# State space layer: where a batch's row adds and statistics stand, and which activation tables it uses

## The reference, cut to what matters

```python
x = x + _L0_ffn_ref(_layernorm(x), ...)        # top-2 experts: two rows per token come back
x = x + _L1_attn_a_ref(_layernorm(x), ...)     # the state space layer
x = x + _L1_ffn_ref(_layernorm(x), ...)

def _layernorm(x, axis=-1, eps=1e-05):
    return (x - mean) / sqrt(var + eps)

def _L1_attn_a_ref(x, W_in, conv_w, conv_b, W_x, W_dt, b_dt, A_log, D, W_out):
    xi, z = split(x @ W_in.T)
    u = silu(causal_conv4(xi) + conv_b)
    Bm, Cm = split(u @ W_x.T)
    delta = softplus(u @ W_dt.T + b_dt)
    dA = exp(delta * -exp(A_log));  dB = delta * Bm
    h_t = dA_t * h_{t-1} + u_t * dB_t;  y_t = sum(h_t * c_t)     # scan over the tokens
    return ((y + u * D) * silu(z)) @ W_out.T
```

## Time and profile before

| | us |
|---|---|
| median of three runs | 4240.26 |
| the three runs | 4235.73, 4240.26, 4248.27 |
| the profiled execution, its own time | 4241.42 |
| its span, first to last instruction | 4239.6 |
| busy in the span: TensorE, VectorE, ScalarE, GpSimd | 3643.4, 2895.8, 1905.3, 1622.4 |
| mean granted TensorE clock | 0.941 |

### The profile page before, as it was taken

How to read it: one execution, slowest core, us unless ns; L and a number is a source line. 1 busy time by engine, 2 the same in 40 slices (tenths; PEclk the granted TensorE clock), 3 DMA queues, 4 the chain that set the end, 5 groups by cost and what they waited for, 6 DMA issues and landing times. The chain is left out here.

```text
span 4239.6 us, 59957 instructions
## 1 busy us (share of the span) xinstructions
PE 3643.4 (86%) x19161; PEld 2603.3 (61%) x19224; DVE 2895.8 (68%) x5457; ACT 1905.3 (45%) x3879; POOL 1622.4 (38%) x1493
## 2 busy tenths in 40 slices
PE   5888877898499999998799578878789899999998
PEld 3555566787488888877688534444556455554666
DVE  5777556565576666646556457787789767676898
ACT  3555543443355555545334244443323266666332
POOL 3776625443566666524544211010101354441000
PEclk8999978999799999998899879899999899999999
DMA  5999802554100000001355400000300444451000
GB/s 134 298 285 264 256 32 86 160 157 155 63 17 17 19 19 22 14 5 49 104 169 168 147 20 18 13 20 1 60 0 11 97 101 112 98 116 34 11 15 15
DMA packets 228873, 358.33 MB, mean 85 GB/s; under 512 B 36482, under 2 KB 132850, under 8 KB 221810
## 3 DMA queue, kind: packets, MB, share of 16 engines
q1 hardware_dynamic: 204038, 265.38, 21.1%
q0 software_dynamic: 24544, 89.36, 8.4%
HBM read 173.82 MB, written 172.20 MB: 82 GB/s over the span
## 5 line engine op out<-in xcount | busy, mean ns | idle before, releaser
L2848 DVE TENSOR_REDUCE ab_nmx<-banks 128x1 f32<-128x512 f32 x512 | 329.2, 684 | 134.3 <-PE banks L2635 131.7
L2779 ACT ACTIVATE ab_pt<-banks 128x512 f32<-128x512 f32 x512 | 283.1, 600 | 159.5 <-PE banks L2645 151.3
L1714 POOL TENSOR_TENSOR lb_pq<-lb_pq,lb_rr 128x512 f32<-128x512 f32 x192 | 206.5, 1079 | 307.0 <-DVE lb_rr L1581 303.9
L1456 ACT ACTIVATE lb_pq<-banks,lb_nmx 128x256 f32<-128x256 f32 x384 | 178.9, 471 | 228.6 <-DVE lb_nmx L1576 225.7
L2645 PE MATMUL banks<-ab_qT,ab_kT 128*128 128x512 f32 x512 | 251.1, 494 | 5.7 <-ACT ab_pt L2779 5.7
L1576 DVE TENSOR_REDUCE lb_nmx<-banks 128x2 f32<-128x512 f32 x192 | 131.2, 683 | 157.0 <-PE banks L1308 155.7
L358 ACT ACTIVATE da_pt<-banks 128x512 f32<-128x512 f32 (+1 forms) x384 | 179.0, 536 | 122.2 <-PE banks L270 117.8
L2635 PE MATMUL banks<-ab_kT,ab_qT 128*128 128x512 f32 x512 | 207.6, 408 | 16.9 <-DVE ab_nmx L2848 12.2
L644 POOL DMA_INDIRECT mb_xi<-moe_ys,moe_b_place x64 | 65.0, 1015 | 388.6 <-DVE mb_uT L2095 340.7
L285 PE MATMUL banks<-da_pt,da_vx 128*64 128x512 f32 (+3 forms) x1024 | 165.7, 469 | 34.0 <-POOL da_pt L578 30.4
L2424 PE MATMUL banks<-w_f_dT,f_hT 128*128 128x256 f32 x768 | 181.2, 387 | 4.0 <-ACT f_hT L2460 4.0
(11 more groups left out here) (532 smaller groups left out, 11230.8 us busy)
## 6 DMA issues: line engine op xcount, KB each, us to landing
moe_xs<-zero SPq DMA_DIRECT2D x71, 512.0 KB, 11.0
moe_ys<-zero SPq DMA_DIRECT2D x71, 512.0 KB, 10.9
moe_a_w_raw<-in_moe_w SPq DMA_DIRECT2D x48, 512.0 KB, 3.9
moe_b_w_raw<-in_moe_w SPq DMA_DIRECT2D x48, 512.0 KB, 3.9
da_spill<-da_hi SPq DMA_DIRECT2D x128, 128.0 KB, 2.4
ab_spill<-ab_hi SPq DMA_DIRECT2D x128, 128.0 KB, 2.4
ab_qT<-ab_spill POOLq DMA_DIRECT2D x32, 392.0 KB, 5.7
ab_kT<-ab_spill POOLq DMA_DIRECT2D x32, 392.0 KB, 5.5
```

What stands on the lines that cost most here:

```text
L1456: nc.scalar.activation(pq[:, n % RING, t, :], ps[:, S_BANK + n % 2, 2 * P * t:2 * P * t + 2 * P], ACT.Exp, bias=nmx[:, n % RING, t:t + 1], ...
L1714: nc.gpsimd.tensor_tensor(pq[:, n % RING, :, :], pq[:, n % RING, :, :], bcast(rr[:, n % RING, :], 2, 2 * P), ALU.mult).then_inc(s_p, 1)
L2779: nc.scalar.activation(pt[:, s % RING, :], ps[:, EXP_BANK + s % 3, :], ACT.Exp, scale=AB_D ** -0.5).then_inc(s_e, 1)
L2848: nc.vector.tensor_reduce(nmx[:, g % 2, col:col + 1], ps[:, MAX_BANK + n % 3, :], op=ALU.max, axis=AX.X, negate=True).then_inc(s_mx, 1)
```

## The change

The job `add` is split: its half k of batch b now stands at -19 + k, that is phases 5 and 6, and the first half waits for the batch's eight gathers. The statistics of the new rows become a job `stats` of their own in phase 7, behind `scan`, where the whole add stood. The statistics of finished rows, which followed `out` 1 in phase 4, become a job `later` at slot 22, that is phase 10 of the next batch, behind `direct` of tile 3; the last batch's come after the loop. `fetch` moves from -18 to -21. `root` computes `exp(-0.5 * ln(var + eps))` into `rstd`, and `scale` has no reciprocal any more. The table set with exponential and logarithm is loaded by name at the start and after each batch's last `u`.

```diff
-    vector_table = [(-17, "add", 0), (-15, "scale", 0), (-12, "conv", 0), ...
-                    ... (-3, "parts", 0), (1, "parts", 1)]
-    pool_table = [(-18, "fetch", 0)]
+    vector_table = [(-19, "add", 0), (-18, "add", 1), (-17, "stats", 0), (-15, "scale", 0), (-12, "conv", 0), ...
+                    ... (-3, "parts", 0), (1, "parts", 1),
+                    (22, "later", 0)]
+    pool_table = [(-21, "fetch", 0)]
...
                 def u(b, m):
...
+                    if m == MB_EC - 1:
+                        nc.scalar.preload_act_table_set("natural_log_exp_and_others")
...
                 def root(b, i):
                     act.wait_ge(s_stats, b + 1)
-                    nc.scalar.activation(core.std[:, b, :], core.mv[:, b, :, 1], ACT.Sqrt, bias=core.eps[:, :],
-                                         scale=1.0).then_inc(s_root, 1)
+                    nc.scalar.activation(core.std[:, b, :], core.mv[:, b, :, 1], ACT.Ln, bias=core.eps[:, :], scale=1.0)
+                    act.drain()
+                    nc.scalar.activation(core.rstd[:, b, :], core.std[:, b, :], ACT.Exp, scale=-0.5).then_inc(s_root, 1)
...
                 act.wait_ge(core.loaded["mb"], core.loads["mb"])
+                nc.scalar.preload_act_table_set("natural_log_exp_and_others")
...
-                def add(b, i):
-                    dve.wait_ge(s_fetch, 16 * TOPK * NT * (b + 1))
-                    for k in range(TOPK):
-                        dve.drain()
-                        choice.add(b, k, fetched).then_inc(s_added, 1)
-                    dve.drain()
+                def add(b, k):
+                    if k == 0:
+                        dve.wait_ge(s_fetch, 16 * TOPK * NT * (b + 1))
+                    choice.add(b, k, fetched).then_inc(s_added, 1)
+                    dve.drain()
+
+                def row_stats(b, i):
                     token_stats(core, dve, b)
                     dve.drain().then_inc(s_stats, 1)
 
+                def later_stats(b, i):
+                    token_stats(core, dve, b)
+
                 def scale(b, i):
                     dve.wait_ge(s_root, b + 1)
-                    nc.vector.reciprocal(core.rstd[:, b, :], core.std[:, b, :])
-                    dve.drain()
...
                 def empty(job):
...
-                        if i == 1:
-                            dve.drain()
-                            token_stats(core, dve, b)
-                            dve.drain()
...
                         if kind != "conv":
                             jobs_of[kind](b, i)
+                dve.drain()
+                later_stats(B - 1, 0)
```

More of the change, by code:

```diff
@@ L1805, in state_space @@
     table += [(3 * i + 4, "turn", i) for i in range(NT)] + [(10, "out", 0), (15, "out", 1)]
-    vector_table = [(-17, "add", 0), (-15, "scale", 0), (-12, "conv", 0), (-11, "conv", 1), (-11, "conv", 2), (-10, "conv", 3),
-                    (-6, "delta", 0), (-5, "scan", 0), (-4, "state", 0), (-4, "cdp", 0), (-3, "parts", 0), (1, "parts", 1)]
-    pool_table = [(-18, "fetch", 0)]
+    vector_table = [(-19, "add", 0), (-18, "add", 1), (-17, "stats", 0), (-15, "scale", 0), (-12, "conv", 0), (-11, "conv", 1), (-11, "conv", 2), (-10, "conv", 3),
+                    (-6, "delta", 0), (-5, "scan", 0), (-4, "state", 0), (-4, "cdp", 0), (-3, "parts", 0), (1, "parts", 1),
+                    (22, "later", 0)]
+    pool_table = [(-21, "fetch", 0)]
     scalar_table = [(-16, "root", 0), (-15, "normal", 0), (-11, "u", 0), (-11, "u", 1), (-10, "u", 2), (-9, "u", 3), (-6, "decay", 0), (-3, "parts", 0), (1, "parts", 1)]
@@ L2190, in finish @@
                     nc.vector.tensor_tensor(gz[b % 2][:, i, :], gz[b % 2][:, i, :], v1[:, :], ALU.mult).then_inc(s_y, 1)
-                jobs_of = {"add": add, "scale": scale, "conv": conv, "delta": step, "scan": scan, "cdp": first_sum, "state": state,
+                jobs_of = {"add": add, "stats": row_stats, "later": later_stats, "scale": scale, "conv": conv, "delta": step, "scan": scan, "cdp": first_sum, "state": state,
                            "parts": parts}
```

## The result

The changed kernel took 4250.59 us (median of 16 runs, 4241.73 to 4257.21), the kernel before 4241.66 (16 runs, 4235.73 to 4249.94): a ratio of 1.0020, 95% interval 1.0013 to 1.0027, or +5.5 to +11.5 us. I had said 4243.6 within 4230 to 4256, and no change that a measurement tells from none (0.3%) as likeliest. It came out so: the increase is clear of the noise but stays under 0.3%. It is some two and a half times my sum of +3.4 us, though. The profiled execution took 4253.90 us (span 4252.1, clock 0.938).

A forecast was written before the change was run, and what follows sets the result against it. A loop of waits, no full engine, was taken to set the period. Gather wait +9.0, moved statistics +1.0, front -5.4 and tail -1.2 make +3.4 us: 4244.8 profiled, 4243.6 as median, range 4230 to 4256.

The forecast's parts named there:

- The gather term: Phase 5: VectorE waits some 6.0 us for gathered rows; 28.2 against 26.74 us to the product, +9.0 in six periods.
- 0.96 throughout: Sign in the profile after: every gather issue on GpSimd takes 0.96 us, none the 1.29 of the last issue before.
- `finish` alone: GpSimd's gather issues: the long ones go away with VectorE's `finish` out of their way; otherwise six periods cost 4.2 us more.
- The moved statistics: Phase 10, before `out`: 2.3 us return, mostly hidden; 0.2 us in each of five periods, +1.0.
- the cover: Phase 10: TensorE's `x` transposes also wait for ScalarE's copies, hiding later-emptied `out`; without it 0.6 us each.
- The front: Stage start to second shift: fewer table loads ahead of the second gather, no reciprocal; -5.4 us (-4.5 to -6.5).
- one table set: ScalarE: five loads of 1.28 us a batch become two; worth nothing more in the six periods, but counting at the front.
- The tail: Last two batches: VectorE paces the last one, so statistics taken from phase 4 are partly gained; -1.2 us.
- (a): Faster rival, phase 5: gathered rows are there when VectorE comes, six periods give -15; 4219.7 us, chance 0.05.
- (b): Slower rival: longer idle TensorE keeps `out` and what follows at low clock, 2 us in six periods; 4255.6, chance 0.12.
- (c): Rival: the table set isn't shared, logarithm and exponential still load, the front loses its gain; 4247, chance 0.03.
- the bounds: Low and high ends of the terms for periods, statistics and front; together said to put the sum at 0 to +10 us.

The follow-up runs named there:

- adds_late: The changed kernel with the two add groups one slot later each (-18 and -17); 4233.76 us, 0.9981 of before.
- own_rows: The changed kernel with fetched rows in buffers free earlier, so gathers no longer wait for the last `conv`; 4224.90 us, 0.9957 of before.
- second pair: Second profiles of the two unchanged programs, the kernel before and the changed kernel; 4248.03 and 4253.90 us.
- first pair: First profiles of the kernel before and the changed kernel; profiled executions 4241.42 and 4253.90 us.
- best: The changed kernel with fetched rows in buffers free earlier and the statistics of finished rows in slot 23 instead of 22; 4221.79 us, 0.9951 of before.
- split_alone: The kernel before with only the adds split and the new rows' statistics in slots of their own, gathers listed at -21; 4253.41 us, 1.0020 of before.
- later_alone: The kernel before with only the statistics of finished rows moved from phase 4 to phase 10 of the next batch; 4251.93 us, 1.0016 of before.

## Why the prediction was right, and where it was off

- **The gather term held.** Predicted 28.2 us from the last `conv` to the product, measured 28.19 in the mean of six periods. The pieces: 0.78 to the first issue, 11.5 to 12.2 from there to the adds (11.80), 15.5 of VectorE's own work (15.65). Six periods make +9.4 against before's mean, where I had +9.0. adds_late and own_rows show that it is this wait: with it gone the stretch takes 25.59 and 23.90.
- **The issues are not 0.96 throughout.** The first profile of after has one of 1.46 in four of the six periods, and there the adds begin 12.8 to 13.0 us behind the `conv` instead of 12.3. It is the fifth, at 2843.92, 0.11 us after VectorE began `direct` (2843.81 to 2844.55). In the fourth period, the short one of 63.80 us, the same issue began 0.23 us ahead of `direct` and was not held up:

```profile
2715.74 0.95 POOL L644 DMA_INDIRECT mb_xi<-moe_ys,moe_b_place  x1 [0.30 <-issue]
2715.97 0.75 DVE L2184 SCALAR_TENSOR_TENSOR mb_v<-w_mb_d,mb_cd,mb_ut 128x512 f32<-128x512 f32 x1
```

The eleven profiles whose gathers run there bear this out: all 49 issues that begin 0.10 to 0.22 us behind the start of a `direct` take 1.36 to 1.47 us, and the 28 others that overlap one (they begin ahead of it, or 0.64 us or more behind its start) take 0.95 to 0.96. The Trainium skill, "SBUF — State Buffer", section "Who interferes with whom", would have it so for an instruction with two SBUF inputs, as `direct` has; these rows agree. The prediction looked for the cause in `finish` alone. In before the seventh issue, at 2710.59, is the longer one, 1.36 us, and stands behind `direct` (2710.37). The last issue of 1.29 did go away, as it said; the one at `direct` moved with `direct` from seventh place to fifth.

- **The moved statistics** were set at +1.0 with the reciprocal's 0.3 in it. The stretch to the first `conv` grew by 0.29 a period, the one to the shift shrank by 0.26, together +0.2 in six. Where the cover is gone they cost 0.6 each, as said; it is gone only in the periods of the higher clock. The prediction counted five periods for them, and four hold the job.
- **The front** was right in size, -5.4 predicted and -5.9 measured (-6.2 by the second pair), but stood under the wrong heading. The split alone gives -4.5 and the tables alone -4.7: both take time out of one chain, and each finds the other's already gone.
- **In the periods** I gave one table set nothing beyond the sum, and in this kernel that is right. The runs showed why: the split makes the loads' 0.66 us invisible. Part by part the change is +8.6 (split), -13.6 (tables) and +7.1 (statistics) by the medians, sum +2, and +8.9 together. One reason that the parts do not add up is that behind the wait the tables are worth 3 us and not 13.
- **The tail is the term that was mis-sized.** I put -1.2; it is +0.9 by the first pair and +3.3 by the second. The tail of before itself moved by 2.4 us from one profile to the other. The step that failed says that VectorE paces the last batch. It doesn't to the end (the last `finish` ends 91 to 92 us behind the last shift in all four): what follows the last `finish` is TensorE's turn and `out`, and the time of that `out` ranges from 3.69 to 6.53 us over the profiles (before 5.38 and 5.15, after 6.34 twice; by the first pair this is the whole +0.9). The count was off too: of the eight sets of these statistics three stood behind the last shift before, and four do now. The statistics ahead of the last `finish` make TensorE wait 2.3 to 2.7 us for it and not 1.66. Of the eight profiles with that job there five have a last `out` of over 6 us, of the six without it none has one over 5.4; and moving that one job gave best 3.2 us of its tail back. How much is the job and how much where the lower clock falls, the runs do not settle: the tail is 112.6 to 117.4 us with the job and 113.4 to 116.5 without.
- **The rivals.** (a) needed the rows earlier; own_rows made them so, with the product 2.7 us sooner than before and 4224.90 us where I had 4219.7. (b), a lower clock, shows in the tail; in the periods the stretch at TensorE grew by 0.29 us and not by 2. (c) did not happen: no load stands ahead of the logarithm. The Trainium skill, "ScalarE: Activation LUTs", section "What ACT_TABLE_LOAD costs", adds a drain of 1.38 us to each load; the load that the changed kernel requests at its start ends at 2424.51 and the exponential begins at 2424.52, so this trace shows none behind the load.
- **The sum.** In the stage its four terms come to +4.9 us by the first pair and +7.6 by the second, where I had +3.4; the remaining 1 to 4 us of the +8.9 are not explained. That the time lies in the range owes something to the range's width, 26 us. Two sums were off by themselves: the bounds add up to -1 to +10 and not 0 to +10, and the terms of (c) to 4246.1 and not 4247.

Open: in three cases even the lower end of the interval lies above what the stage explains, +4.7 us against at most +3.7 for split_alone, +2.5 against +2.1 for later_alone, -23.3 against -26.8 for own_rows. With one profile each I can't say whether that is spread outside the stage or a part of it.

## What to carry to other kernels

Before a consumer is moved up, look at what its producer's start hangs on: these gathers hung on the end of the last convolution, so adds in phase 5 bought nothing but a wait, and the same adds one slot later, or rows in other buffers, did not wait. A saving ahead of a new wait is not a saving: the tables were worth 13 us alone and 3 behind it. And before a few microseconds at a stage's end are given to an edit, compare the same products' durations: here a spell at the lower clock made 2.7 us of difference between two kernels that had waited equally long.

## What the runs showed of the hardware

An issue of a gather was held up or not by a tenth of a microsecond: 1.36 to 1.47 us when it began 0.10 to 0.22 us after `direct`, 0.95 to 0.96 when it began ahead of it. That is most of why both profiles of after have the short period (63.80 and 63.89 us) in the same place among those around it (64.2 to 64.8).

Where TensorE's clock is low is partly the program's own and partly the run's. From 6 us ahead of each of the six shifts to the next first `conv` the two profiles of after show the same clocks within 0.01 (0.50, 0.76, 0.75, 0.75, 0.83, 0.82), and their tails are 117.38 and 117.43 us. The two of before do not: 0.74, 0.79, 0.82, 0.75 and 0.79 from the second window on in the one, 0.83, 0.75, 0.80, 0.83 and 0.76 in the other, with tails of 116.48 and 114.10. What varies most from run to run is the time ahead of the stage, by 15.5 us over fourteen profiles, more than any part of this change is worth.
